# A decoder layer's cross-attention: scores from the context itself, with W_q and W_k folded into one matrix

## The chip, the cores and the metric

The kernel runs on one core of a Trainium2 chip. The metric is the device time of one execution in microseconds. The engines are named as the profile names them: PE (TensorE, matmuls), PEld (PE's weight loads, which run beside its matmuls), DVE (VectorE), ACT (ScalarE), POOL (GpSimd) and SP (SyncE, which issues most DMAs).

## The reference, cut to what matters

One decoder layer: a state-space scan block, a cross-attention over a context of 1601 rows, and a mixture of experts. Every tensor is fp32, the model width is 256. The part that the change touches is the cross-attention, which gets the layer-normed residual stream (2048 rows) as query:

```python
q = jnp.einsum('bse,ae->bsa', query, Wq) + bq
k = jnp.einsum('bse,ae->bsa', key, Wk) + bk        # key is the context, 1601 x 256
v = jnp.einsum('bse,ae->bsa', value, Wv) + bv      # value is the context too
scores = jnp.einsum('bqa,bka->bqk', q, k) / scale  # scale is 16
scores = jnp.where(mask == 0, jnp.float32(-10000000000.0), scores)
attn = jax.nn.softmax(scores, axis=-1)
return jnp.einsum('bqk,bka->bqa', attn, v)
```

## The kernel before, in words

The program has two blocks one after the other, with every engine's instructions written out in order and tied together by semaphores. `scan_block` fills the first 431 us of the span. `attend_and_route` does the rest: a prologue, the attention loop, the dense part of the experts with the routing, and the expert tiles. Nothing of the second block starts before the first has ended.

**Precision.** Large products are made from two fp32r halves. A value x is split as x_hi (rounded to fp32r by ACT when it evicts a PSUM bank) and x_lo = x - x_hi (by DVE, from the same bank). `products` (L1289) then issues three matmuls, hi by hi, hi by lo and lo by hi. Other products, such as the query projection (L1399), are one fp32 matmul, which the trace lists as two matmul records with two weight loads.

**The prologue.** It works through a list, `items` (L771), of PSUM banks to be filled by PE (`take`, L1297), evicted by ACT (L977 to L985) and halved by DVE (L1196 to L1209), always in the order of the list: the three weights, transposed (L1426); the context, transposed in eight pieces (L1434); the keys k = W_k c + b_k in eight pieces (L1437 to L1444); the values in thirteen pieces (L1453). At the start of the keys DVE also does `moments` (L1045): the last four of the sixteen row tiles get their statistics (L1047), and sixteen aggregations give mean and variance (L1051). POOL makes the inverse deviations of all rows from them (L861, L863), and DVE normalises the first query tile (`xn2`, L1186). Between keys and values stands `lead_at`: there every engine runs steps -2 and -1 of the loop, which is the transpose of xn2 (L1392), its eviction (L948), the query product (L1399), and the eviction and halving of q (L953, L1181).

**The attention loop.** `step(i)` is run for i = 0 to 17 on every engine; each handles one tile of 128 query rows in several phases. PE's order in a step is: transposes of the probabilities of tile i-1, groups 0 and 1 (L1321); transposes of the new row tile for the experts (L1344); the first 512 columns of scores of tile i; transposes of groups 2 and 3; transposes of the next query tile (L1392); the other score columns, 512, 512 and 66; the query product for tile i+1 (L1399); the product of the probabilities of tile i-1 with the values, 39 matmuls in thirteen groups of three (L1411). After steps 6, 10 and 14 come the router's logits of four tiles (L1355), after steps 8, 12 and 16 its ranks (L1364, L1366).

DVE's order in a step is: p_lo for the groups of tile i-1 (L1061); the residual of tile i-2 and its statistics (L1154 to L1162); the scores of tile i copied under the mask, in two pieces (L1168); their maximum (L1170); the bias -max/16 (L1172, `nb`); the normalised row of tile i-2 (L1176); q_lo of tile i+1 (L1181); xn2 of tile i+2 (L1186); parts of the routing in some steps. ACT evicts p_hi (L928), the transposes and q_hi (L953), and then does the exponential of tile i with the row sum as accumulator output (L963), which waits for `nb` and for which PE waits before the transposes of the next step (L1310).

SP loads the mask tiles (L815), the first of them once the transposed context has left the memory that the mask takes. POOL adds the value bias, fills the score buffer for the mask, and does the two small operations for the deviations (L901, L903).

## Time and profile before

| what | value |
|---|---|
| median of 3 runs | 826.59 us (825.5 to 828.36) |
| the profiled execution | 824.91 us |
| its span in the profile | 823.1 us, 11006 instructions |
| mean granted clock of PE | 0.883 |
| PE busy | 637.5 us (77%), 3196 matmuls |
| PEld busy | 400.5 us (49%) |
| DVE busy | 601.7 us (73%), 1009 |
| ACT busy | 421.6 us (51%), 744 |
| POOL busy | 453.6 us (55%), 324 |

The span is the profile's time from the first to the last instruction; the execution's own time is 1.8 us longer. Times in the rows are microseconds from the start of the span, and a row of the timeline merges like instructions that follow each other (x8 is eight of them). The duration of a matmul includes its way through the array, so the pace of a row of matmuls is read from their starts. What stands in brackets at the end of a row is the engine's idle time before it, and what ended it. The granted clock is given as a share of 2.4 GHz.

### The profile page before, as it was taken

Reading aid. Unit: us, or ns where it says so; the run is one execution under the profiler, and the core shown is the slowest. Engines: PE = TensorE matmul, PEld = TensorE weight load, DVE = VectorE, ACT = ScalarE, POOL = GpSimd, SP = SyncE. Lnnn points to the kernel's source line nnn. Section 1 sums busy time; section 2 is a strip of 40 time slices with the busy share of each in tenths; the row PEclk is TensorE's granted clock in tenths of the full one; section 3 lists DMA queues with packets and bytes.
Section 4 is the critical chain, followed back from the end, with each engine's and each line's share of the span. In section 5 each row is a group of like instructions: output and inputs, shape, how many; then the busy total and the mean of one; then the engine's idle time right before and its main releaser. Section 6 shows DMA issues by size and latency. Waiting matters only on the chain. (4 is left out here: it accounts for less than half of the span.)

```text
span 823.1 us, 11006 instructions
## 1 busy us (share of the span) xinstructions
PE 637.5 (77%) x3196; PEld 400.5 (49%) x3196; DVE 601.7 (73%) x1009; ACT 421.6 (51%) x744; POOL 453.6 (55%) x324
## 2 busy tenths in 40 slices
PE   4569857996499854653379799999999988899950
PEld 2123212341134210210038699998989964588840
DVE  5767787799977999997987566668777665344316
ACT  2557898587966898553425334434334220244420
POOL 3058698798986989995942212212334236046550
PEclk9789986999689985675589899999999999999985
DMA  7143342334334344464202113313413049655418
GB/s 195 34 109 92 76 99 64 97 87 102 88 79 99 78 105 103 100 186 103 67 0 87 41 61 111 131 46 128 144 54 106 15 133 325 139 152 150 134 27 300
DMA packets 70584, 87.43 MB, mean 106 GB/s; under 512 B 18197, under 2 KB 47320, under 8 KB 70526
## 3 DMA queue, kind: packets, MB, share of 16 engines
q1 hardware_dynamic: 54782, 67.26, 30.7%
q10 hardware_dynamic: 12000, 11.28, 4.3%
q0 software_dynamic: 3744, 8.19, 2.9%
q8 instruction: 27, 0.44, 0.2%
q14 instruction: 31, 0.25, 0.1%
HBM read 36.54 MB, written 18.66 MB: 67 GB/s over the span
## 5 line engine op out<-in xcount | busy, mean ns | idle before, releaser
L262 POOL TENSOR_TENSOR b_in<-u_rep,b_rep 128x1024 f32<-128x1024 f32 x128 | 299.0, 2361 | 72.3 <-DMA dt_rep<-dt 30.1
L477 DVE TENSOR_TENSOR_SCAN h<-ps,hlast,b_in 128x512 f32<-128x512 f32 x256 | 306.3, 1265 | 22.0 <-ACT ps L383 11.1
L383 ACT ACTIVATE ps<-dt_rep,neg_a 128x512 f32<-128x512 f32 x256 | 171.4, 686 | 75.5 <-DVE h L477 60.2
L615 PE MATMUL ps<-h,pick 128*32 128x512 f32 x512 | 84.9, 742 | 70.4 <-DVE h L477 70.0
L512 PE MATMUL ps<-xnT,w_in 128*128 128x512 f32 x128 | 67.8, 677 | 17.6 <-ACT xnT L308 10.3
L615 PEld LDWEIGHTS ps<-h,pick 128*32 128x32 f32 x512 | 11.0, 118 | 134.9 <-DVE h L477 130.5
L917 POOL DMA_INDIRECT rows_by_token<-yt,yrow x46 | 44.9, 975 | 52.4 <-DVE yrow L1254 25.3
L1061 DVE TENSOR_TENSOR p_lo<-ps,p_hi 128x512 fp32r<-128x512 f32 x64 | 35.1, 587 | 42.8 <-ACT p_hi L928 42.6
L1292 PE MATMUL ps<-v_hi,p_hi 128*128 128x256 f32 x208 | 59.7, 287 | 1.2 <-DVE x_res L1158 1.2
L1292 PE MATMUL ps<-v_hi,p_lo 128*128 128x256 f32 x208 | 58.5, 281 | 0.0
L1292 PE MATMUL ps<-v_lo,p_hi 128*128 128x256 f32 x208 | 58.5, 281 | 0.0
L928 ACT ACTIVATE p_hi<-ps 128x512 fp32r<-128x512 f32 x64 | 30.0, 516 | 45.4 <-PE ps L1321 45.4
L512 PEld LDWEIGHTS ps<-xnT,w_in 128*128 128x128 f32 x128 | 26.1, 214 | 55.3 <-issue 37.6
L895 POOL TENSOR_TENSOR x_res<-x_res,bv 128x256 f32<-128x256 f32 x16 | 11.7, 734 | 68.5 <-ACT pr L963 68.5
L1292 PE MATMUL ps<-k_hi,q_hi 128*128 128x512 f32 (+1 forms) x128 | 48.4, 378 | 1.0 <-ACT v_hi L983 1.0
L901 POOL TENSOR_TENSOR rstd3s<-mv3s,eps 128x1 f32<-128x1 f32 x16 | 3.1, 191 | 81.6 <-DVE mv3s L1162 81.6
L1292 PE MATMUL ps<-k_lo,q_hi 128*128 128x512 f32 (+1 forms) x128 | 46.9, 366 | 0.0
L1292 PE MATMUL ps<-k_hi,q_lo 128*128 128x512 f32 (+1 forms) x128 | 46.6, 367 | 0.0
L527 PE MATMUL ps<-xp,conv_d 128*128 128x512 f32 x96 | 43.6, 598 | 0.0
L1537 PE MATMUL ps<-w_exp,xT 128*128 x184 | 43.5, 379 | 0.0
L963 ACT ACTIVATE pr<-sc,nb 128x1601 f32<-128x1601 f32 x16 | 26.2, 1640 | 28.1 <-DVE nb L1172 28.1
L1292 PEld LDWEIGHTS ps<-v_hi,p_hi 128*128 128x128 f32 x208 | 39.3, 189 | 1.4 <-DVE x_res L1158 1.4
(228 smaller groups left out, 1289.3 us busy)
## 6 DMA issues: line engine op xcount, KB each, us to landing
u_rep<-u SPq DMA_DIRECT2D x256, 64.0 KB, 2.0
dt_rep<-dt SPq DMA_DIRECT2D x248, 64.0 KB, 2.0
mask_sb<-in_mask_BxSxS_ik_dram SPq DMA_DIRECT2D x16, 800.5 KB, 4.5
xt<-rows_by_expert SPq DMA_DIRECT2D x46, 129.0 KB
rows_by_token<-pad ACTq DMA_DIRECT2D x4, 1024.0 KB, 5.1
yb<-rows_by_token SPq DMA_DIRECT2D x4, 512.0 KB, 5.2
yb<-rows_by_token ACTq DMA_DIRECT2D x4, 512.0 KB, 5.9
x_res<-in_x_dram SPq DMA_DIRECT2D x1, 1536.0 KB, 8.7
```

The costliest lines, as they stand in the source:

```text
L262: pool.tensor_tensor(b_in[:, (t - 1) % NB:(t - 1) % NB + 2, :], u_rep[:, n % 2, j - 1:j + 1, :], b_rep[:, q % 2, g, :].unsqueeze(1).to_bro ...
L383: act.activation(psA[:, t % NDA, :], dt_rep[:, n % 2, j, :], ACT.Exp, scale=neg_a[:, k:k + 1]).then_inc(exp_ready, 1)
L477: dve.tensor_tensor_scan(h[:, QC * (s % NH) + j, :], psA[:, t % NDA, :], b_in[:, t % NB, :], hlast[:, k:k + 1], ALU.mult, ALU.add).then_in ...
L512: last = pe.matmul(psF[:, m % 2, :], w_in[:, n, part * DI + m * P:part * DI + (m + 1) * P], xnT[:, n, :], start=(n == 0), stop=(n == KE - 1))
L527: last = pe.matmul(psF[:, m % 2, :], conv_d[:, m, n, :], xp[:, m, n:n + CH], start=(n == 0), stop=(n == NTAP - 1))
L615: last = pe.matmul(psY[32 * j:32 * j + 32, :], pick[:, :], h[:, QC * (s % NH) + j, :], start=False, stop=(g == NG - 1))
L917: pool.indirect_dma_start(y_dram[:, :], bass.IndirectOffsetOnAxis(ap=yrow[:, 2 * s + a:2 * s + a + 1], axis=0), yt[:, s % YT, a, :], None, ...
L928: act.activation(p_hi[:, (i - 1) % 2, a:b, :], psP[g % 2][:, 0:(b - a) * P], ACT.Copy).then_inc(pthi_ready, 1)
L963: act.activation(pr[:, par, 0:SK], sc[:, par, :], ACT.Exp, bias=nb[:, par:par + 1], scale=SCALE, accum_out=rs[:, par:par + 1]).then_inc(ex ...
L1061: dve.tensor_tensor(p_lo[:, (i - 1) % 2, a:b, :], psP[g % 2][:, 0:(b - a) * P], p_hi[:, (i - 1) % 2, a:b, :].bitcast(F32), ALU.subtract).t ...
L1292: mm = pe.matmul(out, stat[a], mov[b], start=first and n == 0, stop=last and n == 2)
L1537: last = pe.matmul(psG[i % 2][:, a * 2 * FI:(a + 1) * 2 * FI], xT[:, i % 2, cols], w_all[:, ds(e, 1), wcols].rearrange("p a n -> p (a n)") ...
```

## The change

The scores are taken as (W_k^T (W_q x + b_q)) . c instead of q . k. With `wqk` = W_q^T W_k (made by PE in fp32 from the weights as loaded, without transposes) and W_k^T b_q as the bias of the new query, c is the transposed context, which the kernel holds in halves already. The term q . b_k is the same for a whole row of scores and leaves the softmax unchanged; it is still computed for each row (`qb`, a product with the vector W_q^T b_k and a sum along the row on DVE) and goes through max and bias as (qb - (max + qb))/16. What the diff does:

- `items` loses the transposes of W_q and W_k and the eight pieces of keys, and gets two items after the context: `wqk`, and `fold`, which holds W_q^T b_k on all partitions, b_q . b_k, and W_k^T b_q. Both are evicted by ACT alone.
- The 66 last context columns are also kept as whole fp32 (`c_end`, two small copies by DVE), and the last 66 score columns are two fp32 matmuls in place of six fp32r ones.
- The query is evicted as fp32 `q` by two ACT instructions; a third, from `q`, makes `q_hi`. DVE makes `q_lo` with one subtraction of 256 columns. PE waits for `q` where it waited for `q_lo` before it reuses the bank of the query.
- DVE gets in each tile, between the masked copy and the maximum, a scalar_tensor_tensor of 257 columns with an accumulator output, and after the maximum a tensor_tensor of one column, on which `nb` waits.
- `moments` stands where the fold items come, after the halving of the context. `c_hi` and `c_lo` stay in memory through the loop where `k_hi` and `k_lo` were.

The diff, cut to its core:

```diff
@@ -702,13 +702,14 @@
         with ExitStack() as first:
-            k_hi, k_lo = sb("k_hi", [P, KE, SKP], F32R, first), sb("k_lo", [P, KE, SKP], F32R, first)
+            c_hi, c_lo = sb("c_hi", [P, KE, SKP], F32R, first), sb("c_lo", [P, KE, SKP], F32R, first)
+            c_end = sb("c_end", [P, KE, SCOL[-1][1] - SCOL[-1][0]], F32, first)
+            fold = sb("fold", [P, 2 + DM + KE], F32, first)
             v_hi, v_lo = sb("v_hi", [P, KC, DM], F32R, first), sb("v_lo", [P, KC, DM], F32R, first)
             xqT = sb("xqT", [P, KE, P], F32, first)
-            q_hi, q_lo = sb("q_hi", [P, 2, KE, P], F32R, first), sb("q_lo", [P, 2, KE, P], F32R, first)
+            q, q_hi, q_lo = sb("q", [P, 2, KE, P], F32, first), sb("q_hi", [P, 2, KE, P], F32R, first), sb("q_lo", [P, 2, KE, P], F32R, first)
+            qb, full, prod = sb("qb", [P, 1], F32, first), sb("full", [P, 1], F32, first), sb("prod", [P, DM + 1], F32, first)
             with ExitStack() as prep:
-                c_hi, c_lo = sb("c_hi", [P, KE, SKP], F32R, prep), sb("c_lo", [P, KE, SKP], F32R, prep)
-                wk_hi, wk_lo = sb("wk_hi", [P, KE, DM], F32R, prep), sb("wk_lo", [P, KE, DM], F32R, prep)
                 wv_hi, wv_lo = sb("wv_hi", [P, KE, DM], F32R, prep), sb("wv_lo", [P, KE, DM], F32R, prep)
@@ -759,19 +762,21 @@
-        wq_items = [(bank[0].rearrange("p (k n) -> p k n", k=KE), wqT[:, :, :], None, None)]
-        wkv_items = [(bank[n].rearrange("p (k n) -> p k n", k=KE), hi[:, :, :], lo[:, :, :], None)
-                     for n, (hi, lo) in ((1, (wk_hi, wk_lo)), (2, (wv_hi, wv_lo)))]
-        ctx_items = [(bank[(3 + n) % 8][:, 0:b - a], c_hi[:, k, a:b], c_lo[:, k, a:b], None)
+        wv_items = [(bank[0].rearrange("p (k n) -> p k n", k=KE), wv_hi[:, :, :], wv_lo[:, :, :], None)]
+        ctx_items = [(bank[(1 + n) % 8][:, 0:b - a], c_hi[:, k, a:b], c_lo[:, k, a:b], c_end[:, k, :] if b == SKP else None)
                      for n, (k, (a, b)) in enumerate([(k, ab) for ab in KCOL for k in range(KE)])]
-        k_items = [(bank[(3 + n) % 8][:, 0:b - a], k_hi[:, m, a:b], k_lo[:, m, a:b], bk[:, m:m + 1])
-                   for n, (m, (a, b)) in enumerate([(m, ab) for ab in KCOL for m in range(KE)])]
+        fold_items = [(bank[1].rearrange("p (k n) -> p k n", k=KE), wqk[:, :, :], None, None),
+                      (bank[2][:, 0:1 + DM + KE], fold[:, 0:1 + DM + KE], None, None)]
         VBANKS = (3, 4, 5, 7, 0, 1, 2)
         v_items = [(bank[VBANKS[n % 7]][:, 0:DM], v_hi[:, n, :], v_lo[:, n, :], None) for n in range(KC)]
-        items = wq_items + wkv_items + ctx_items + k_items + v_items
+        items = wv_items + ctx_items + fold_items + v_items
         lead_at = len(items) - len(v_items)
-        bank_of = ([0, 1, 2] + [(3 + j) % 8 for j in range(len(ctx_items))] + [(3 + j) % 8 for j in range(len(k_items))]
-                   + [VBANKS[j % 7] for j in range(len(v_items))])
+        bank_of = [0] + [(1 + j) % 8 for j in range(len(ctx_items))] + [1, 2] + [VBANKS[j % 7] for j in range(len(v_items))]
+        fold_at = len(wv_items) + len(ctx_items)
+
+        def halved(n):
+            return len([lo for _, _, lo, _ in items[:n + 1] if lo is not None])
+
         cv_src = [bank[k][:, 0:KS * P].rearrange("p (t n) -> p t n", t=KS) for k in range(KE)]
@@ -814,7 +819,7 @@
-            sp_.wait_ge(prep_ps, 3 + len(ctx_items))
+            sp_.wait_ge(prep_ps, fold_at)
             for i in range(NT):
@@ -950,8 +955,11 @@
                     for m in range(KE):
-                        act.activation(q_hi[:, (i + 1) % 2, m, :], psA[:, (KE + m) * P:(KE + m + 1) * P], ACT.Identity,
-                                       bias=bq[:, m:m + 1]).then_inc(qhi_ready, 1)
+                        last = act.activation(q[:, (i + 1) % 2, m, :], psA[:, (KE + m) * P:(KE + m + 1) * P], ACT.Identity,
+                                              bias=fold[:, DM + 1 + m:DM + 2 + m])
+                    last.then_inc(q_ready, 1)
+                    act.wait_ge(q_ready, i + 2)
+                    act.activation(q_hi[:, (i + 1) % 2, :, :], q[:, (i + 1) % 2, :, :], ACT.Copy).then_inc(qhi_ready, 1)
                 if on(i, 0):
@@ -974,15 +982,13 @@
             act.wait_ge(b_in, 48)
-            for n, (src, hi, lo, bias) in enumerate(items):
+            for n, (src, hi, lo, whole) in enumerate(items):
                 if n == lead_at:
+                    act.wait_ge(prep_hi, lead_at)
                     step(-2)
...
                 act.wait_ge(prep_ps, n + 1)
-                if bias is None:
-                    act.activation(hi, src, ACT.Copy).then_inc(prep_hi, 1)
-                else:
-                    act.activation(hi, src, ACT.Identity, bias=bias).then_inc(prep_hi, 1)
+                act.activation(hi, src, ACT.Copy).then_inc(prep_hi, 1)
             for i in range(NT + 2):
@@ -1041,6 +1047,7 @@
             dve.memset(x3[:, :, 0:KS - 1], 0.0)
+            dve.memset(xn2[:, :, DM:DM + 1], 1.0)
@@ -1166,24 +1173,31 @@
                         dve.copy_predicated(sc[:, par, a:b], mask_sb[:, par, a:b], psS[:, a:b]).then_inc(masked, 1)
+                    if i == 0:
+                        dve.wait_ge(prep_hi, lead_at)
+                    dve.wait_ge(xn2_ready, i + 1)
+                    dve.scalar_tensor_tensor(prod[:, :], xn2[:, par, :], 1.0, fold[:, 0:DM + 1], ALU.mult, ALU.mult,
+                                             accum_out=qb[:, :]).then_inc(qb_ready, 1)
                     dve.wait_ge(masked, 2 * i + 2)
                     dve.reduce_max(mx[:, par:par + 1], sc[:, par, :], AXX).then_inc(dve_link, 1)
+                    dve.wait_ge(qb_ready, i + 1)
                     dve.wait_ge(dve_link, i + 2)
-                    dve.tensor_scalar(nb[:, par:par + 1], mx[:, par:par + 1], -SCALE, None, ALU.mult).then_inc(nb_ready, 1)
+                    dve.tensor_tensor(full[:, :], mx[:, par:par + 1], qb[:, :], ALU.add).then_inc(full_ready, 1)
+                    dve.wait_ge(full_ready, i + 1)
+                    dve.tensor_scalar(nb[:, par:par + 1], qb[:, :], full[:, 0:1], SCALE, ALU.subtract, ALU.mult).then_inc(nb_ready, 1)
                 if on(i, -2):
...
                 if on(i, 1):
-                    dve.wait_ge(qhi_ready, KE * (i + 2))
-                    for m in range(KE):
-                        dve.scalar_tensor_tensor(q_lo[:, (i + 1) % 2, m, :], psA[:, (KE + m) * P:(KE + m + 1) * P], bq[:, m:m + 1],
-                                                 q_hi[:, (i + 1) % 2, m, :].bitcast(F32), ALU.add, ALU.subtract).then_inc(qlo_ready, 1)
+                    dve.wait_ge(qhi_ready, i + 2)
+                    dve.tensor_tensor(q_lo[:, (i + 1) % 2, :, :], q[:, (i + 1) % 2, :, :],
+                                      q_hi[:, (i + 1) % 2, :, :].bitcast(F32), ALU.subtract).then_inc(qlo_ready, 1)
                 if on(i, 2):
...
                         dve.wait_ge(xq_ps, i + 1)
-                    dve.tensor_scalar(xn2[:, par, :], x_res[:, i + 2, :], mv[:, i + 2, 0:1], rstd[:, i + 2:i + 3],
+                    dve.tensor_scalar(xn2[:, par, 0:DM], x_res[:, i + 2, :], mv[:, i + 2, 0:1], rstd[:, i + 2:i + 3],
                                       ALU.subtract, ALU.mult).then_inc(xn2_ready, 1)
@@ -1193,20 +1207,19 @@
-            for n, (src, hi, lo, bias) in enumerate(items):
+            for n, (src, hi, lo, whole) in enumerate(items):
+                if n == fold_at:
+                    moments()
                 if lo is None:
                     continue
-                if n == 3 + len(ctx_items):
-                    moments()
                 if n == lead_at:
...
                 dve.wait_ge(prep_hi, n + 1)
-                if bias is None:
-                    dve.tensor_tensor(lo, src, hi.bitcast(F32), ALU.subtract).then_inc(prep_lo, 1)
-                else:
-                    dve.scalar_tensor_tensor(lo, src, bias, hi.bitcast(F32), ALU.add, ALU.subtract).then_inc(prep_lo, 1)
+                if whole is not None:
+                    dve.tensor_copy(whole, src[:, 0:whole.shape[1]])
+                dve.tensor_tensor(lo, src, hi.bitcast(F32), ALU.subtract).then_inc(prep_lo, 1)
             for i in range(NT + 2):
@@ -1325,14 +1338,17 @@
                     if first == 0:
-                        pe.wait_ge(qlo_ready, KE * (i + 1))
+                        pe.wait_ge(qlo_ready, i + 1)
                     for s in range(first, last_):
...
                         for k in range(KE):
-                            last = products(psS[:, a:b], (q_hi[:, i % 2, k, :], q_lo[:, i % 2, k, :]),
-                                            (k_hi[:, k, a:b], k_lo[:, k, a:b]), k == 0, k == KE - 1)
+                            if s == len(SCOL) - 1:
+                                last = pe.matmul(psS[:, a:b], q[:, i % 2, k, :], c_end[:, k, :], start=(k == 0), stop=(k == KE - 1))
+                            else:
+                                last = products(psS[:, a:b], (q_hi[:, i % 2, k, :], q_lo[:, i % 2, k, :]),
+                                                (c_hi[:, k, a:b], c_lo[:, k, a:b]), k == 0, k == KE - 1)
                         if s % 2 == 1:
@@ -1378,7 +1394,7 @@
                     if on(i, 0):
-                        pe.wait_ge(qlo_ready, KE * (i + 1))
+                        pe.wait_ge(q_ready, i + 1)
                     x3_transposed(i - 3)
@@ -1386,7 +1402,7 @@
                     if i >= 0:
-                        pe.wait_ge(qlo_ready, KE * (i + 1))
+                        pe.wait_ge(q_ready, i + 1)
                     pe.wait_ge(xn2_ready, i + 2)
@@ -1396,7 +1412,7 @@
                         for k in range(KE):
-                            last = pe.matmul(psA[:, (KE + m) * P:(KE + m + 1) * P], wqT[:, k, m * P:(m + 1) * P], xqT[:, k, :],
+                            last = pe.matmul(psA[:, (KE + m) * P:(KE + m + 1) * P], wqk[:, k, m * P:(m + 1) * P], xqT[:, k, :],
                                              start=(k == 0), stop=(k == KE - 1))
@@ -1419,12 +1435,11 @@
             pe.wait_ge(w_in, 48)
-            for m in range(3):
-                out_ = take()
-                for a in range(KE):
-                    for k in range(KE):
-                        last = pe.transpose(out_[:, k, a * P:(a + 1) * P], w_raw[:, m, a, k * P:(k + 1) * P], ident[:, :])
-                last.then_inc(prep_ps, 1)
+            out_ = take()
+            for a in range(KE):
+                for k in range(KE):
+                    last = pe.transpose(out_[:, k, a * P:(a + 1) * P], w_raw[:, 2, a, k * P:(k + 1) * P], ident[:, :])
+            last.then_inc(prep_ps, 1)
@@ -1434,28 +1449,39 @@
-            for g, (a, b) in enumerate(KCOL):
-                pe.wait_ge(prep_lo, 2 + KE * (g + 1))
-                for m in range(KE):
-                    out_ = take()
-                    for k in range(KE):
-                        last = products(out_, (wk_hi[:, k, m * P:(m + 1) * P], wk_lo[:, k, m * P:(m + 1) * P]),
-                                        (c_hi[:, k, a:b], c_lo[:, k, a:b]), k == 0, k == KE - 1)
-                    last.then_inc(prep_ps, 1)
+            out_ = take()
+            for k in range(KE):
+                for a in range(KE):
+                    last = pe.matmul(out_[:, k, :], w_raw[:, 0, a, k * P:(k + 1) * P], w_raw[:, 1, a, :], start=(a == 0), stop=(a == KE - 1))
+            last.then_inc(prep_ps, 1)
+            pe.wait_ge(b_in, 48)
+            out_ = take()
+            for a in range(KE):
+                pe.matmul(out_[:, 0:DM], bk[:, a:a + 1].to_broadcast([P, P]), w_raw[:, 0, a, :], start=(a == 0), stop=(a == KE - 1))
+            for a in range(KE):
+                pe.matmul(out_[:, DM:DM + 1], bk[:, a:a + 1].to_broadcast([P, P]), bq[:, a:a + 1], start=(a == 0), stop=(a == KE - 1))
+            for m in range(KE):
+                for a in range(KE):
+                    last = pe.matmul(out_[:, DM + 1 + m:DM + 2 + m], w_raw[:, 1, a, m * P:(m + 1) * P], bq[:, a:a + 1],
+                                     start=(a == 0), stop=(a == KE - 1))
+            last.then_inc(prep_ps, 1)
             for c in range(KC):
...
                     pe.wait_ge(prep_hi, q_last + 1)
-                    pe.wait_ge(prep_lo, q_last)
+                    if halved(q_last):
+                        pe.wait_ge(prep_lo, halved(q_last))
+                    pe.wait_ge(prep_hi, lead_at)
                     step(-2)
                     step(-1)
+                pe.wait_ge(prep_lo, halved(fold_at))
                 out_ = take()
...
             pe.wait_ge(prep_hi, len(items))
-            pe.wait_ge(prep_lo, len(items) - 1)
+            pe.wait_ge(prep_lo, halved(len(items)))
             for i in range(NT + 2):
```

## Rows read from the trace of the kernel before

**Rows 1.** Windows: busy us (count) of PE, PEld, DVE, ACT, POOL; clock; DMA.
```profile
459.50:667.00 207.50, 199.69 (x1419) 183.59 (x1419) 146.69 (x336) 75.85 (x158) 56.74 (x74) 0.98 0.26 87
...
431.80:447.00 15.20, 14.08 (x86) 12.28 (x86) 12.77 (x40) 9.67 (x19) 4.36 (x12) 1.00 0.31 117
```

**Rows 2.** Timeline of the prologue, all engines: start, us, engine, line, operation.
```profile
432.53 0.60 ACT L983 ACTIVATE wqT<-ps 128x512 f32<-128x512 f32 x1 [10.59 <-PE ps L1426]
...
433.14 3.00 PE L1434 MATMUL ps<-ident,c_raw 128*128 128x128 f32 x26
...
433.65 0.69 DVE L1207 TENSOR_TENSOR wk_lo<-ps,wk_hi 128x512 fp32r<-128x512 f32 x1 [1.75 <-ACT wk_hi L983]
...
434.86 4.07 DVE L1207 TENSOR_TENSOR c_lo<-ps,c_hi 128x512 fp32r<-128x512 f32 x8
...
438.84 1.40 DVE L1047 BATCH_NORM_STATS2 stats<-x_res 128x6 f32<-128x256 f32 x4
...
441.89 2.93 POOL L863 TENSOR_TENSOR attn_rstd<-attn_rstd,attn_powers 128x16 f32<-128x16 f32 x1
...
446.64 0.41 DVE L1186 TENSOR_SCALAR xn<-x_res,attn_mv,attn_rstd 128x256 f32<-128x256 f32 x1
...
447.19 0.41 PE L1392 MATMUL ps<-ident,xn 128*128 128x128 f32 x2 [1.26 <-DVE xn L1186]
...
448.08 1.16 PE L1399 MATMUL ps<-xqT,wqT 128*128 128x128 f32 x8 [0.47 <-ACT xqT L948]
```

**Rows 3.** Timeline of one tile of the attention loop, all engines.
```profile
507.76 0.90 PEld L1321 LDWEIGHTS ps<-ident,pr 128*128 128x128 f32 x8
...
513.69 2.00 DVE L1168 COPY_PREDICATED sc<-mask_sb,ps 128x1024 f32<-128x1024 int32 x2
...
515.72 1.82 DVE L1170 TENSOR_REDUCE mx<-sc 128x1 f32<-128x1601 f32 x1
...
517.58 0.15 DVE L1172 TENSOR_SCALAR nb<-mx 128x1 f32<-128x1 f32 x1
...
517.66 0.42 DVE L1176 TENSOR_SCALAR xn<-x_res,mv3s,rstd3s 128x256 f32<-128x256 f32 x1
...
517.77 1.64 ACT L963 ACTIVATE pr<-sc,nb 128x1601 f32<-128x1601 f32 x1 [1.54 <-DVE nb L1172]
...
519.31 0.18 ACT L963 ACTIVATION_READ_ACCUMULATOR pr<-sc,nb 128x1 f32 x1
...
519.91 0.90 PEld L1321 LDWEIGHTS ps<-ident,pr 128*128 128x128 f32 x8
```

**Rows 4.** Timeline where the loop's last tile begins.
```profile
660.20 1.64 ACT L963 ACTIVATE pr<-sc,nb 128x1601 f32<-128x1601 f32 x1 [6.04 <-DVE nb L1172]
...
661.98 0.86 PEld L1321 LDWEIGHTS ps<-ident,pr 128*128 128x128 f32 x8 [0.68 <-ACT pr L963]
```

**Rows 5.** Waits in the loop: engine, line, releaser: us, times, longest.
```profile
PEld ps L1321 <- ACT pr L963: 4.6, 2, 3.9
```

**Rows 6.** PE timeline of another tile: a 66-column product, the query product, the logits.
```profile
590.23 0.28 PE L1292 MATMUL ps<-k_lo,q_hi 128*128 128x66 f32 x1
...
590.78 1.14 PE L1399 MATMUL ps<-xqT,wqT 128*128 128x128 f32 x8
...
596.37 1.86 PE L1355 MATMUL ps<-r_w,x 128*128 128x16 f32 x16
```

**Rows 7.** Groups by line and form: busy us, mean ns, then idle.
```profile
L1244 DVE SCALAR_TENSOR_TENSOR x_res<-xn,w_same,x_res 128x256 f32<-128x256 f32 x16 | 7.6, 477 | 0.0
```

**Rows 8.** Timeline of the scan's end: four fp32 products of 256 columns.
```profile
429.02 1.99 PE L540 MATMUL ps<-w_out,zs 128*128 128x256 f32 x8 [0.81 <-DVE zs L434]
```

**Rows 9.** Windows around PE's wait in the first tile, columns as in rows 1.
```profile
467.00:469.00 2.00, 0.00 (x0) 0.00 (x0) 1.46 (x5) 1.31 (x1) 0.00 (x0) 0.61 0.81 330
...
474.00:475.00 1.00, 1.00 (x8) 0.99 (x8) 0.00 (x0) 0.33 (x1) 0.00 (x0) 0.86 0.00 0
```

**Rows 10.** Timeline of the same place.
```profile
469.47 1.97 PE L1321 MATMUL ps<-ident,pr 128*128 128x128 f32 x8 [3.73 <-ACT pr L963]
```

18 lines of the change are left out of this document (10 added, 8 removed).

## The prediction

> **What bounds the kernel now.** I first split the attention block by windows [rows 1]. In the loop, from 459.5 to 667 us, PE is busy 199.7 of 207.5 us and DVE only 146.7, so the loop is PE's. In the prologue, 431.8 to 447, PE is busy 14.1 of 15.2 us, but DVE 12.8, so it may be either's. Busy shares don't settle what ends last in a stage; the timelines do.
>
> In the prologue [rows 2] PE ends the context's transposes at 433.14 + 3.00 = 436.14, issues the keys until 447.19 - 1.26 = 445.93, and stands 1.26 us for `xn2` (DVE, 446.64). Beside the keys runs a second chain: DVE halves the context (434.86 to 438.93), does the moments (from 438.84), POOL raises to the power -1/2 (441.89 to 444.82, one instruction of 2.93 us), DVE normalises. That chain would have had `xn2` ready soon after 444.8; DVE was then still halving keys. So the keys end last, but the moments chain ends only 1.8 us before them. This is what I look for: the work removed covers something almost as long.
>
> In the loop [rows 3] a tile takes 519.91 - 507.76 = 12.15 us on PE. A second chain closes on itself in each tile: probability transposes, p_hi, p_lo, masked copy, maximum, `nb`, exponential, next transposes. Where this chain is known to bind [rows 4], PE starts 661.98 - 660.20 = 1.78 us after the exponential starts. In the tile of rows 3 the exponential starts at 517.77, so PE could have started at 519.55 and started at 519.91: **slack 0.37 us**. The waits say the same: PE's weight loads stood for the exponential in 2 tiles only, the first and the last [rows 5]. Of the 15 intervals between the 16 tiles' probability transposes, 3 hold the logits (1.86 us of PE work on top [rows 6]), one is the slow tile after the first, 2 are ends, and 9 are like the one shown within 0.05 us or, where routing comes in on DVE, somewhat longer.
>
> **Part 1, the prologue.** Removed on PE: eight weight transposes and the keys. From the pace of row L1434 (26 in 3.00 us, 0.115 each) the transposes are 0.9 us; the keys are 445.93 - 436.14 = 9.8 us. Added: six fp32 products of 256 columns and six of one column. Four of the former took 1.99 us [rows 8], so six are at most 3.0 us; one of the latter costs at least its two weight loads and at most the 0.28 us of two records at L1399's pace (1.14 us for 8 [rows 6]), 1.7 us in all. PE would then be ready for `xn2` at 445.93 - 0.9 - 9.8 + 4.7 = 439.9. By PE's work alone the prologue gains 7.3 us.
>
> But `xn2` isn't there. DVE's first operation now starts when ACT's first eviction ends, 432.53 + 0.60 = 433.13, and one halving instead of two lies before the context's. Two took 434.86 - 433.65 = 1.21, so the context's halving starts at 433.15 + 0.60 = 433.75, 1.1 us earlier. The two `c_end` copies of 66 columns take back 0.15 us each at `nb`'s price of 0.15 for a tiny operation [rows 3]; at most 0.28. The rest of the chain is unchanged and now has no cover: the moments begin 0.8 us earlier, POOL ends at 444.0, `xn2` starts at 444.1 instead of 446.64. **Gain 2.5 us** (2.3 to 2.8), with PE standing idle from 439.9 to about 444.6. ACT loses two weight and eight key evictions and gets two; it has nothing on this path. SP's mask loads start 0.9 us earlier and nobody waits for them.
>
> **What that idle time costs.** In the first tile PE stops at 469.47 - 3.73 = 465.74 [rows 10], and the granted clock falls from full (2.4 GHz) to half (1.2 GHz) at about 467.4, since its mean is 0.61 from 467 to 469 [rows 9]. PE works again at 469.47 and the clock is back at about 474.3 (mean 0.86 from 474 to 475). A wait of 3.7 us thus brought 4.8 us at half clock. The new wait is 4.7 us, so I expect the same: half clock until 444.6 + 4.8 = 449.4. The dense work (query product, then values) starts 0.9 us after the transposes as now (448.08 against 447.19), so 3.9 us are worked at half clock, which loses 1.95, and 0.15 for the transposes: **2.1 us given back**. Bounds: 0, if the clock holds, and 3.3 us, if the half clock lasts half as long again. Part 1 nets -0.4 us.
>
> **Part 2, the loop on PE.** Six fp32r matmuls of 66 columns start 0.11 us apart ((590.78 - 590.23)/5 [rows 6]): 0.66. The new two are four records. The eight 128-column records of L1399 take 1.14 with 0.28 for the last, so 0.12 each; with 66 columns they are no slower: 0.48. **PE saves 0.2 us a tile** (0.15 to 0.4). PE's earlier release by `q` instead of `q_lo` is worth nothing: q_lo was ready long before PE came to it.
>
> **Part 3, the loop on DVE.** Between the masked copy and the exponential come two operations. The scalar_tensor_tensor's nearest row is L1244, two fp32 operands in SBUF, 256 columns: 0.477 [rows 7]. It waits for nothing, so it overlaps its predecessor by the 0.07 us that DVE rows show when no wait is between (`nb` ends at 517.73, the next has started at 517.66 [rows 3]), and its successor by as much, where the maximum today starts 0.03 after the copy (513.69 + 2.00, 515.72): net 0.29. No row of DVE has an accumulator output. ACT's has one, and there it leaves a second instruction of 0.18 us that ends 0.08 after the main one ([rows 3], 519.31 + 0.18 against 517.77 + 1.64). I add 0.07; the bounds are 0 and 0.18. The Trainium skill says the same of DVE: an operation that writes its accumulator is two instructions (VectorE: DVE Perf Modes, Two Vector instructions with no wait between them). The one-column addition costs `nb`'s 0.15 + 0.04 for the wait: 0.19, as `nb` to exponential shows (517.77 - 517.58). **D = 0.29 + 0.07 + 0.19 = 0.55 us** later at the exponential; bounds 0.48 and 0.75.
>
> q_lo becomes one operation instead of two, but stands behind `nb` and shortens nothing there. The third ACT instruction for the query falls into ACT's wait of 1.54 us for `nb` [rows 3]; it reads 256 columns, and even at the 0.60 of the prologue's 512-column eviction [rows 2] none of it shows. If `nb` came 1 us earlier, it would.
>
> **The sum of the loop.** D exceeds the slack of 0.37, so the exponential becomes the last to arrive in ordinary tiles. Per interval: the 9 ordinary ones and the slow tile, taken as ordinary, D - 0.37 = +0.18 each, 10 x 0.18 = +1.8. The 3 with logits keep PE as bound: -0.6. The first end: D - 0.2 = +0.35. The last: D = +0.55. Together **+2.1 us**. With part 1: **+1.7 us** on the profiled 824.91, so 826.6. That execution lies 1.7 us under the median of the runs, 826.59; for the median I add the same: 828.3. A measurement of this kernel can tell about 0.3% (2.5 us) from no change.
>
> **Rivals.**
> *The clock holds* through PE's wait (or falls near its end): the loss of 2.1 goes, sum -0.4, 826.2. Against it: the fall came 1.7 us into a shorter wait [rows 9, 10]. It is no change too.
> *PE stays the bound* (faster). If D is 0.37 or less, or the slack is larger than the rows show, 0.2 x 16 = -3.2 us in the loop; with part 1 at -0.4 to -2.5 the time is 821 to 823. Against it: the maximum, `nb` and exponential stand one behind the other with no gap to take up 0.48 us between them.
> *The whole of the keys is gained* (faster): the prologue gives 7.3 instead of 2.5, with no wait and no lost clock: -7.3 + 2.1 = -5.2, 821.4. That needs the moments chain off the path; against it, POOL's one instruction of 2.93 us starts after DVE's whole halving.
> *DVE's new operation is slow* (slower). The place is between copy and maximum. If two fp32 SBUF operands with a running sum went at half the pace of L1244, it would last 0.95, D would be 1.03 and the loop 10 x 0.66 - 0.6 + 0.83 + 1.03 = +7.9; sum +7.5, 834.1. It decides from D = 0.65 on: 10 x 0.28 - 0.6 + 0.45 + 0.65 = +3.3, less 0.4. For it: nothing in the trace shows this operation with its sum. Against: L1244 has the two operands and takes 0.477, where `nb`'s 0.15 and 256 columns at the maximum's pace (1.82/1601 = 1.14 ns) make 0.44. The Trainium skill has this rule: such an operation with two SBUF sources that aren't bf16 has half the throughput (Vector Engine (DVE) Microarchitecture Reference, Points that are easy to get wrong); L1244 contradicts it without a sum, and no row here shows it with one.
>
> **How the numbers follow.** Forecast and the clock rival, both within 2.5 us: 0.38 and 0.17. Slow DVE work, or the forecast's terms at their upper bounds (D 0.75: 10 x 0.38 - 0.6 + 0.55 + 0.75 = +4.5; 3.3 lost to the clock: +0.8; sum +5.3): 0.30. PE as bound 0.09, whole gain 0.06. So faster 0.15, same 0.55, slower 0.30. The range leaves out the whole gain, the strongest PE-bound case and doubled DVE price: from 823.5 (D at 0.48, PE's saving 0.4, 2.8 gained in the prologue and the clock held make 10 x 0.11 - 1.2 + 0.1 + 0.5 - 2.8 = -2.3, or 824.3, with 0.8 for the runs' own spread) to 832.0 (the terms at their upper bounds).
>
> **What would show it.** In the profile after: `xn2` at 444.1, PE idle for some 4.5 us before it, granted clock 0.5 in the window behind it; the value products' start at about 447; PE's weight loads of the probabilities released by the exponential in 10 or more tiles instead of 2; a tile of 12.3 us, the maximum starting some 0.4 us after the copy's end; four records between the last 512 columns and the query product. I'm wrong if the tile is 11.95 us (PE still binds) or over 12.5 us (D was too small), and if PE finds `xn2` ready.

## The result and the profile after

The kernel after takes 828.31 us (median of 20 runs, 825.64 to 832.93) against 825.45 (20 runs, 822.67 to 828.36): **ratio 1.0041, 95% interval 1.0029 to 1.0054**, 3.4 us slower (2.4 to 4.5). A second set of runs of the same program gave 1.0038 [1.0019, 1.0056], where 1.0025 to 1.0045 was expected. The profiled execution took 827.98 us. Head of its page:

```profile
span 826.3 us, 10924 instructions
...
PE 636.8 (77%) x3132; PEld 395.5 (48%) x3132; DVE 601.4 (73%) x1035; ACT 422.8 (51%) x752; POOL 453.8 (55%) x324
```

I read it by stretches: the prologue (first weight transpose to first score product on PE), the first scores (to the first probability transpose), the loop (to the last tile's first transpose), and what lies before and behind.

| us | start | prologue | first scores | loop | behind |
|---|---|---|---|---|---|
| before | 431.81 | 27.75 | 9.91 | 192.51 | 161.17 |
| after | 434.85 | 27.13 | 10.26 | 194.92 | 159.09 |
| after, second set | 432.48 | 27.34 | 10.25 | 195.00 | 160.35 |

Start and behind hold the same work in every kernel here and still wander between executions (431.8 to 434.9, and 159.1 to 162.9). The three stretches between make **-0.62 + 0.35 + 2.41 = +2.14 us**.

**The prologue**, timeline of the kernel after (start, us, engine, line), to be set beside [rows 2]:

```profile
436.81 3.67 DVE L1222 TENSOR_TENSOR c_lo<-ps,c_hi 128x512 fp32r<-128x512 f32 x6
...
441.06 1.40 DVE L1054 BATCH_NORM_STATS2 stats<-x_res 128x6 f32<-128x256 f32 x4
441.11 1.03 PE L1465 MATMUL ps<-bq,w_qkv_raw 128*128 128x1 f32 x8
...
444.10 2.93 POOL L868 TENSOR_TENSOR attn_rstd<-attn_rstd,attn_powers 128x16 f32<-128x16 f32 x1
447.06 0.41 DVE L1200 TENSOR_SCALAR xn<-x_res,attn_mv,attn_rstd 128x256 f32<-128x256 f32 x1 [3.41 <-POOL attn_rstd L868]
447.62 0.66 PE L1408 MATMUL ps<-ident,xn 128*128 128x128 f32 x2 [5.49 <-DVE xn L1200]
448.82 2.07 PE L1415 MATMUL ps<-xqT,wqk 128*128 128x128 f32 x8 [0.53 <-ACT xqT L953]
```

PE is done at 442.1 and stands 5.49 us for `xn2`; what the keys covered is now the path. Behind the wait the query product takes 2.07 us instead of 1.16 [rows 2], and the windows show why (columns as in [rows 1], the granted clock third from the end): half clock, 1.2 of 2.4 GHz, where [rows 1] have 1.00:

```profile
446.00:448.00 2.00, 0.38 (x2) 0.29 (x2) 0.41 (x1) 0.00 (x0) 1.93 (x7) 0.51 0.00 0
448.00:452.00 4.00, 3.47 (x17) 3.19 (x16) 0.00 (x0) 1.42 (x4) 0.22 (x3) 0.50 0.00 0
452.00:454.00 2.00, 2.00 (x15) 2.00 (x15) 1.37 (x4) 0.77 (x4) 0.00 (x0) 0.78 0.00 0
```

**An ordinary tile**, to be set beside [rows 3]:

```profile
504.09 2.00 DVE L1175 COPY_PREDICATED sc<-mask_sb,ps 128x1024 f32<-128x1024 int32 x2
...
505.98 0.41 DVE L1179 SCALAR_TENSOR_TENSOR prod<-xn,fold 128x257 f32<-128x257 f32 x1
506.32 0.08 DVE L1179 DVE_READ_ACCUMULATOR prod<-xn,fold 128x1 f32 x1
506.32 1.82 DVE L1182 TENSOR_REDUCE mx<-sc 128x1 f32<-128x1601 f32 x1
...
508.24 0.16 DVE L1185 TENSOR_TENSOR full<-mx,qb 128x1 f32<-128x1 f32 x1
508.43 0.21 DVE L1187 TENSOR_SCALAR nb<-qb,full 128x1 f32<-128x1 f32 x1
...
508.68 1.64 ACT L971 ACTIVATE pr<-sc,nb 128x1601 f32<-128x1601 f32 x1 [1.76 <-DVE nb L1187]
```

From the copy's start to the exponential's are 508.68 - 504.09 = 4.59 us, against 4.08 before: **D = 0.51 us**. The maximum now starts 0.23 after the copy's end instead of 0.03, and from its end to the exponential are 0.54 instead of 0.23. Waits of the loop, to be set beside [rows 5]:

```profile
PEld ps L1334 <- ACT pr L971: 7.5, 10, 4.5
...
PE ps L1334 <- DVE base L1117: 2.1, 2, 1.0
```

The exponential holds PE in 10 tiles instead of 2; `base`, the last routing operation that uses the shared PSUM bank, holds it for 2.1 us in all where it was 0.8.

**The loop's 15 intervals** between first probability transposes, after minus before:

| kind | how many | before | after | change, sum |
|---|---|---|---|---|
| the slow one behind the first tile | 1 | 14.27 | 13.97 | -0.30 |
| ordinary | 6 | 11.94 to 12.34 | 11.98 to 12.36 | +0.37 |
| with logits on PE | 3 | 13.87 to 13.89 | 13.78 to 13.83 | -0.18 |
| with routing on DVE, first of a pair | 2 | 13.02, 13.06 | 13.37, 13.37 | +0.65 |
| with routing on DVE, second of a pair | 2 | 12.80, 12.76 | 13.46, 13.48 | +1.38 |
| the last | 1 | 11.86 | 12.35 | +0.49 |

A pair is two intervals in a row, over which DVE does the routing of four tiles. Of +2.41 us, 2.03 fall into the four intervals with routing. **What binds there**, first the kernel before, then after (timelines of the first pair; the last row is PE at the beginning of the second interval):

```profile
557.65 0.18 ACT L963 ACTIVATION_READ_ACCUMULATOR pr<-sc,nb 128x1 f32 x1
...
558.39 1.04 PE L1321 MATMUL ps<-ident,pr 128*128 128x128 f32 x8
558.53 1.53 DVE L1081 CAST at_f<-top_at 128x8 f32<-128x8 uint32 x1
558.59 1.45 POOL L897 MEMSET sc<- 128x1601 f32 x1
...
560.63 1.28 DVE L1061 TENSOR_TENSOR p_lo<-ps,p_hi 128x512 fp32r<-128x512 f32 x2
...
561.37 0.93 PE L1321 MATMUL ps<-ident,pr 128*128 128x128 f32 x5 [0.35 <-DVE p_lo L1061]
...
568.85 1.64 ACT L963 ACTIVATE pr<-sc,nb 128x1601 f32<-128x1601 f32 x1 [1.38 <-DVE nb L1172]
...
572.45 0.63 PE L1321 MATMUL ps<-ident,pr 128*128 128x128 f32 x4 [0.40 <-DVE base L1110]
```

```profile
560.88 0.18 ACT L971 ACTIVATION_READ_ACCUMULATOR pr<-sc,nb 128x1 f32 x1
...
561.12 1.09 PE L1334 MATMUL ps<-ident,pr 128*128 128x128 f32 x8
...
561.56 1.70 DVE L1088 CAST at_f<-top_at 128x8 f32<-128x8 uint32 x1
561.80 1.44 POOL L902 MEMSET sc<- 128x1601 f32 x1
563.30 0.36 DVE L1092 TENSOR_TENSOR hot<-ids,at_f 128x64 f32<-128x64 f32 x2
...
563.84 1.28 DVE L1068 TENSOR_TENSOR p_lo<-ps,p_hi 128x512 fp32r<-128x512 f32 x2
...
564.58 0.93 PE L1334 MATMUL ps<-ident,pr 128*128 128x128 f32 x5 [0.74 <-DVE p_lo L1068]
...
572.56 1.64 ACT L971 ACTIVATE pr<-sc,nb 128x1601 f32<-128x1601 f32 x1 [1.59 <-DVE nb L1187]
...
576.14 0.63 PE L1334 MATMUL ps<-ident,pr 128*128 128x128 f32 x4 [1.02 <-DVE base L1117]
```

A cast of 8 columns takes 1.5 to 1.7 us, and in both kernels it ends with POOL's memset: 560.06 against 560.04, 563.26 against 563.24. The Trainium skill gives the rule (SBUF — State Buffer, SBUF: two separate sides): VectorE, in its two-port mode, and GpSimd lock a shared pair of ports for a whole instruction, and the other waits. The trace agrees as to the waiting; in which mode the cast ran no row says. But by these records the cast begins ahead of the memset that holds it, by 0.06 us before and 0.24 after. The memset follows the end of the exponential (561.06 + 0.74), so the cast, all of DVE's stream behind it, and the first `p_lo` stand at a fixed distance behind the exponential. Before, the exponential had ended 0.56 us ahead of PE's transposes (557.83 against 558.39), now 0.06. So `p_lo` starts 2.72 us behind the transposes instead of 2.24, 0.48 later, nearly all of D, and PE waits 0.74 us for it instead of 0.35. In the same tile D comes a second time: the next exponential starts 11.44 us behind those transposes instead of 10.46. What is late by then stays late until `base`, for which PE waits 1.02 instead of 0.40 us. The two intervals together grow by 1.01 us, which is twice D.

### The profile page after: what moved, and what is told of

Read it like the earlier page. It is cut to its first block and busy times, and to the rows that moved or that the text cites. A ratio compares the mean times of both kernels' runs of the same rounds, so it can differ in the third digit from the quotient of the medians.

```text
span 826.3 us, 10924 instructions
## 1 busy us (share of the span) xinstructions
PE 636.8 (77%) x3132; PEld 395.5 (48%) x3132; DVE 601.4 (73%) x1035; ACT 422.8 (51%) x752; POOL 453.8 (55%) x324
## 5 line engine op out<-in xcount | busy, mean ns | idle before, releaser
L615 PE MATMUL ps<-h,pick 128*32 128x512 f32 x512 | 87.9, 766 | 68.9 <-DVE h L477 68.5
L1305 PE MATMUL ps<-c_hi,q_hi 128*128 128x512 f32 x96 | 41.1, 428 | 1.0 <-ACT v_hi L991 1.0
L612 PE MATMUL ps<-xc,skip_d 128*128 128x512 f32 x32 | 23.4, 821 | 22.0 <-DVE zs L434 22.0
L1305 PEld LDWEIGHTS ps<-v_lo,p_hi 128*128 128x128 f32 x208 | 39.3, 189 | 0.0
```

What stands on the lines that cost most here:

```text
L615: last = pe.matmul(psY[32 * j:32 * j + 32, :], pick[:, :], h[:, QC * (s % NH) + j, :], start=False, stop=(g == NG - 1))
L1305: mm = pe.matmul(out, stat[a], mov[b], start=first and n == 0, stop=last and n == 2)
```

## The experiments

All ratios are against the kernel before, of five rounds each; stretches are from each run's profile.

**1. Is it the new addresses?** The kernel before, with `xn2` one column wider, as the change makes it.

```diff
-            xn2 = sb("xn2", [P, 2, DM], F32, second)
+            xn2 = sb("xn2", [P, 2, DM + 1], F32, second)
```

> The kernel before, with xn2 one column wider (257) and otherwise the same, so that every SBUF tile allocated behind it sits 8 bytes further on, as in the kernel after. Theory A (the change costs time only through DVE's chain in the loop and the wait in the prologue): ratio 1.000 within 0.1%. Rival B (the scan block, which the change doesn't touch, slowed by the shifted tiles, as its 434.8 us against 431.8 in the two profiles could suggest): +0.15 to +0.4%, and a scan block that ends near 434.8 us in the profile.

Measured: 825.07 us, ratio 1.0002 [0.9985, 1.0019], loop 192.77. The shift explains nothing. Its prologue took 29.26 us, though, 1.5 more than before's with the same instructions: the clock fell behind the wait of 1.25 us, which it had not done in the profile of before.

**2. The uncovered chain.** The kernel after, with the moments first on DVE.

```diff
+            moments()
             for n, (src, hi, lo, whole) in enumerate(items):
-                if n == fold_at:
-                    moments()
```

> The kernel after, with DVE's moments ahead of the halving of the context instead of behind it. Theory A: POOL's 2.93 us instruction now runs beside the halving; the halving ends some 1.5 us later, xn2 is ready 4.5 us earlier than in the kernel after, PE's wait of 5.5 us shrinks to 1 us, the granted clock stays at 1.00 through the prologue, which saves a further 2 us. 6 to 7 us faster than after, so 3 to 4 us faster than before: ratio 0.9955 to 0.997. Rival C (PE's wait in the prologue covers nothing that matters, because DVE's halving or the values' evictions take its place): no more than 2 us faster than after, ratio 1.001 to 1.004. Rival D (the wait counts, the clock doesn't): 4.5 us, ratio 0.9985.

Measured: 821.09 us, ratio **0.9948 [0.9929, 0.9968]**, prologue 21.06 us instead of 27.13. Its timeline:

```profile
435.95 2.93 POOL L868 TENSOR_TENSOR attn_rstd<-attn_rstd,attn_powers 128x16 f32<-128x16 f32 x1
...
440.24 0.41 DVE L1200 TENSOR_SCALAR xn<-x_res,attn_mv,attn_rstd 128x256 f32<-128x256 f32 x1
...
441.56 0.41 PE L1407 MATMUL ps<-ident,xn 128*128 128x128 f32 x2 [0.68 <-ACT fold L991]
...
442.50 1.16 PE L1414 MATMUL ps<-xqT,wqk 128*128 128x128 f32 x8 [0.53 <-ACT xqT L953]
```

`xn2` is ready at 440.65, before PE comes to it at 441.56, and the clock stays full in this execution. The prologue takes 6.7 us less than before's, nearly the 7.3 that the prediction gave for PE alone (6.0 us of work and the wait of 1.3). The ratio came out a little better than the 0.9955 to 0.997 expected; the loop of this execution is 1.4 us shorter than that of after, by the two things named in experiment 4.

**3. The same edit in the kernel before**, where the keys should cover that chain.

```diff
+            moments()
             for n, (src, hi, lo, bias) in enumerate(items):
...
-                if n == 3 + len(ctx_items):
-                    moments()
```

> The kernel before with the moments ahead of the halving of the weights, nothing else. My theory: in the kernel before the keys end last and only cover the moments chain, so freeing that chain takes away at most PE's wait of 1.26 us for xn2 and moves nothing else in the loop: ratio 0.998 to 1.000, xn2 on DVE still behind the halving of the last keys. Rival: the order of the moments is worth as much without the change (the 6 us that it gave in the kernel after, a gain from the clock and from something in the loop): ratio 0.993 to 0.995; then the change has nothing to do with it.

Measured: 826.82 us, ratio 1.0009 [0.9992, 1.0027]. PE's wait is the same to the hundredth:

```profile
447.22 1.32 DVE L1208 SCALAR_TENSOR_TENSOR k_lo<-ps,bk,k_hi 128x512 fp32r<-128x512 f32 x3 [0.61 <-ACT k_hi L985]
448.46 0.40 DVE L1186 TENSOR_SCALAR xn<-x_res,attn_mv,attn_rstd 128x256 f32<-128x256 f32 x1
449.01 0.41 PE L1391 MATMUL ps<-ident,xn 128*128 128x128 f32 x2 [1.26 <-DVE xn L1186]
```

DVE was on the keys until then, whatever the moments did. The edit even costs something here: the halvings stand behind the moments, and `xn2` starts 15.51 us into the block (448.46 - 432.95) instead of 14.83. So the edit of 2 is worth nothing without the change: the gain there is the change's own, and only the new order lets it through.

**4. The clock.** The kernel after, with 11 fp32 products of 256 columns, whose result nobody reads, in PE's wait.

```diff
+                    pe.wait_ge(prep_hi, 4)
+                    pe.wait_ge(prep_lo, 4)
+                    for r in range(11):
+                        pe.matmul(bank[3][:, 0:DM], w_raw[:, 0, 0, 0:P], w_raw[:, 1, 0, :], start=True, stop=True)
                     pe.wait_ge(prep_hi, lead_at)
                     step(-2)
```

> The kernel after, with eleven fp32 matmuls of 256 columns (results not used, into a free bank) put into PE's wait for xn2 in the prologue, 4.7 us of work in a wait of 5.5. If the half clock behind that wait costs what the forecast said (Theory A: 2.1 us), the granted clock reads 1.00 from 440 to 456 us, xn2 and its transposes stand where they stood in after, the values are through some 2 us earlier, ratio 1.0015 to 1.0025 against before. Rival F (the clock falls there by chance anyway, in before too, since the profile of the padded kernel before shows 0.93 from 435 to 459 where before shows 1.00): on average less than 1 us gained, ratio 1.003 to 1.004.

Measured: 824.28 us, ratio 0.9984 [0.9973, 0.9996]; the granted clock is 1.00 throughout the prologue, which takes 25.22 us: **the clock costs 27.13 - 25.22 = 1.9 us** there. The total gained 4.0 us, more than the 2 expected. In the profiled execution two things outside the prologue make up the rest; whether they are in the other runs too isn't known. The slow interval took 13.28 instead of 13.97 (clock 0.93 instead of 0.87 from 459 to 485), and the first interval with routing 12.27 instead of 13.37, because the cast this once got by:

```profile
558.42 0.34 DVE L1088 CAST at_f<-top_at 128x8 f32<-128x8 uint32 x1
...
558.67 1.47 POOL L902 MEMSET sc<- 128x1601 f32 x1
559.07 1.10 DVE L1094 COPY xn<-at_f 128x4 f32<-128x4 f32 x1
```

The small copy behind it is then the one held (to 560.17, memset to 560.14), and nobody waits for that. The same happened once in experiment 2. In the other 26 of 28 such places of all the profiles the cast was held. The start of the cast doesn't tell which it will be: by the records' starts to the nanosecond, it got by 0.239 and 0.249 us ahead of the memset, and was held at 0.237, at 0.249 (experiment 6) and at 0.255. **A hold costs this interval 1.1 us, and the pair 0.9**, since the next interval took 13.61 and 13.62 us in the two executions instead of 13.46. What it costs in the kernel before isn't shown, as the cast was held in each of its profiles.

**5. DVE's new work in the loop.** The kernel after without it; left out is the term q . b_k, the same for a whole row of scores.

```diff
-                    dve.scalar_tensor_tensor(prod[:, :], xn2[:, par, :], 1.0, fold[:, 0:DM + 1], ALU.mult, ALU.mult,
-                                             accum_out=qb[:, :]).then_inc(qb_ready, 1)
...
-                    dve.tensor_tensor(full[:, :], mx[:, par:par + 1], qb[:, :], ALU.add).then_inc(full_ready, 1)
-                    dve.wait_ge(full_ready, i + 1)
-                    dve.tensor_scalar(nb[:, par:par + 1], qb[:, :], full[:, 0:1], SCALE, ALU.subtract, ALU.mult).then_inc(nb_ready, 1)
+                    dve.tensor_scalar(nb[:, par:par + 1], mx[:, par:par + 1], -SCALE, None, ALU.mult).then_inc(nb_ready, 1)
```

> The kernel after without the term q.b_k: the scalar_tensor_tensor and the one-column addition between the masked copy and nb are gone, nb is -max/16 as before. What is left out is the same for a whole row of scores and leaves the softmax as it is. Theory A: the exponential comes 0.5 us earlier in each tile, PE is the bound again with 0.25 us less work a tile: a tile of 11.9 us against 12.26 in after and 12.17 in before; first to last transposes 4 to 5 us shorter than in after; 5 to 6 us faster than after, ratio 0.997 to 0.998 against before. Rival E (the two operations are hidden, the loss is elsewhere): as after, ratio 1.004.

Measured: 824.89 us, ratio 0.9994 [0.9976, 1.0013], loop 191.26, 3.7 us less than after. Ordinary intervals like the one shown fall to 12.03, those with routing to 13.05 and 12.82, as before. So D makes the loop's loss, in both kinds of interval. An ordinary tile of 11.9 was expected, since PE's saving was taken as 0.25 us; 12.03 against 12.17 before make it 0.13. The ratio gained 1 to 2 us less than expected.

**6. Twice the suspect.** The kernel after, with the scalar_tensor_tensor issued twice, the first into tiles that nobody reads.

```diff
+                    dve.wait_ge(qb2_ready, i)
+                    dve.scalar_tensor_tensor(prod2[:, 0:DM + 1], xn2[:, par, :], 1.0, fold[:, 0:DM + 1], ALU.mult, ALU.mult,
+                                             accum_out=qb2[:, 0:1]).then_inc(qb2_ready, 1)
                     dve.scalar_tensor_tensor(prod[:, :], xn2[:, par, :], 1.0, fold[:, 0:DM + 1], ALU.mult, ALU.mult,
```

> The kernel after, with the scalar_tensor_tensor and its accumulator output issued twice between masked copy and maximum. Theory A: the chain binds, so each of the 12 intervals without logits grows by the whole price of one, 0.34 to 0.42 us, a tile of 12.6 to 12.7 us, first to last transposes 4.5 to 5.5 us longer than in after: ratio 1.0095 to 1.011 against before. Rival E (DVE has room there): ratio 1.004 to 1.005.

Measured: 831.26 us, ratio 1.0063 [1.0047, 1.0080], loop 198.61 (+3.7). Ordinary intervals take 12.62 instead of 12.26: with no slack left each 0.35 us on DVE (the second starts 0.35 behind the first) is 0.36 of the tile. A pair with routing grows by 0.72 us, twice the 0.36. The intervals with logits gave nothing (13.74 against 13.78 in the first; PE still binds there), and the whole is less than the 4.5 to 5.5 us expected, by the loop and more so by the ratio (1.0095 to 1.011 expected).

**7. The exact term off the path** (r8). Moments first, and the scalar_tensor_tensor of the next tile at the end of the step, behind `xn2`.

```diff
-                    dve.scalar_tensor_tensor(prod[:, :], xn2[:, par, :], 1.0, fold[:, 0:DM + 1], ALU.mult, ALU.mult,
-                                             accum_out=qb[:, :]).then_inc(qb_ready, 1)
...
+                if on(i, 1):
...
+                    dve.scalar_tensor_tensor(prod[:, :], xn2[:, (i + 1) % 2, :], 1.0, fold[:, 0:DM + 1], ALU.mult, ALU.mult,
+                                             accum_out=qb[:, :]).then_inc(qb_ready, 1)
```

> All of the change kept, with two moves: the moments first (as in r2_moments), and the scalar_tensor_tensor for tile i+1 at the end of DVE's step i, in the 2.3 us in which DVE waits for the transposes of the probabilities. Only the one-column addition, 0.19 us, stays between maximum and exponential, less than the slack of 0.37. Theory A: PE binds in ordinary tiles, 12.0 to 12.05 us a tile as in r3_no_qb and r4_both, ratio 0.990 to 0.992 against before, level with r4_both. Rival H (the operation at the step's end pushes q_lo or the next p_lo): the tile is 12.2 us or more, ratio 0.994 or more.

Measured: 821.16 us, ratio 0.9937 [0.9913, 0.9961]. Less than expected: ordinary intervals fell to 12.08, but those with routing took 13.39 and 13.50, as in after. DVE's operation now stands in front of the routing. In the first of a pair the cast begins later, 0.08 us behind the memset, and ends with it all the same; the first `p_lo` starts 2.74 us behind PE's transposes, where it was 2.72 in after. In the second of a pair PE waits up to 1.3 us for `base` instead of 1.0.

**8. The 66 columns.** Six fp32r products again instead of the two fp32 ones, in the kernel after (r6) and in one without DVE's work and with the moments first (r4, the edits of 2 and 5 together; r9 with the six products).

```diff
-                            if s == len(SCOL) - 1:
+                            if s == len(SCOL):
```

> The kernel after, with the last 66 score columns as six fp32r matmuls again instead of two in fp32. Theory A (DVE's chain binds in ordinary tiles): PE's 0.2 us more a tile are taken from its wait for the exponential, a tile stays at 12.26 us, the three intervals with logits grow by 0.2; in all 0.3 to 1 us slower than after, ratio 1.0045 to 1.0055 against before. Rival G (PE still binds in after): 0.2 x 16 = 3.2 us slower, ratio 1.008.

> The last two edits together: moments first, and without the term q.b_k. Theory A: the two savings add, since they lie in different stretches: 11 to 12.5 us faster than after, 8 to 9.5 us faster than before, ratio 0.9885 to 0.990. Rivals C and E: the smaller of the savings is missing, ratio 0.996 or more.

> r4_both (moments first, no q.b_k), with the last 66 score columns as six fp32r matmuls again. Here PE binds in ordinary tiles, so the price of the 66 columns shows where in r6_six it was hidden. Theory A: the six records take 0.66 us where the four take 0.39 to 0.46, a tile of 12.2 us instead of 12.02, first to last transposes 2.5 to 3.5 us longer than r4_both's 190.5, ratio 0.993 to 0.995 against before. Rival I (the saving of the two fp32 matmuls is eaten elsewhere on PE): 12.05 us a tile, ratio 0.990 to 0.991.

Measured: r6 828.06 us, ratio 1.0021 [1.0004, 1.0038], loop 195.63 (+0.7), ordinary tile 12.26 as with the two. r4 817.50, ratio 0.9904 [0.9881, 0.9928], loop 190.51. r9 819.61, ratio 0.9932 [0.9910, 0.9954], loop 193.49: **+3.0 us**. Of these, 1.1 are the slow interval, 14.60 against 13.51, with the clock at 0.87 and 0.93 from 459 to 485 in the two executions, mostly the clock's and not the edit's. The other 1.9 are **0.2 in each of the six ordinary intervals and the three with logits**; the four with routing and the last one gained nothing. That the total fell into the 2.5 to 3.5 us expected is luck in part. PE's saving counts where PE binds and is hidden where the exponential or the routing does. In the kernel after it is mainly the intervals with logits that show it (13.96 against 13.81). By the ratio, r6 missed what was expected (1.0045 to 1.0055): its median is that of after, 828.06 against 828.31, and a difference of 0.7 us is too small to show there.

**9. Addresses once more.** The twelve score products of 512 columns took 2.89 us in after (525.95 to 528.84) and 2.82 before, with the same shapes; over all tiles of a profile the means are 2.88 and 2.84. So in r10 the kernel of r4 got its new tiles placed behind those that the kernel had before.

```diff
-            c_end = sb("c_end", [P, KE, SCOL[-1][1] - SCOL[-1][0]], F32, first)
-            fold = sb("fold", [P, 2 + DM + KE], F32, first)
             v_hi, v_lo = sb("v_hi", [P, KC, DM], F32R, first), sb("v_lo", [P, KC, DM], F32R, first)
...
+            q_hi, q_lo = sb("q_hi", [P, 2, KE, P], F32R, first), sb("q_lo", [P, 2, KE, P], F32R, first)
+            q = sb("q", [P, 2, KE, P], F32, first)
+            c_end = sb("c_end", [P, KE, SCOL[-1][1] - SCOL[-1][0]], F32, first)
```

> r4_both with the new tiles (q, c_end, fold) placed behind the old ones in SBUF, so that the values and the halves of the query lie in the same order as in before. In after and r4_both the twelve 512-column score matmuls of a tile take 2.88 us from the first to the next operation, in before 2.82. Rival J (the place in SBUF sets that pace): 2.82 us and a tile of 11.95 us, 1 us faster than r4_both. Rival K (it isn't the place): 2.88 us and the same time as r4_both, ratio 0.990.

Measured: 813.43 us, ratio **0.9862 [0.9838, 0.9887]**, the fastest version here, 11 us under before and 15 under after. Ordinary intervals fall from 12.02 to 11.94, the loop to 189.47. Its products run from the first to the second row below in 2.84 us:

```profile
529.33 0.48 PE L1297 MATMUL ps<-c_hi,q_hi 128*128 128x512 f32 x1
...
532.17 0.55 PE L1340 MATMUL ps<-c_end,q 128*128 128x66 f32 x4
532.56 1.11 PE L1407 MATMUL ps<-xqT,wqk 128*128 128x128 f32 x8
```

That is also their mean over its tiles, the pace of before. r6 and r9, with six products for the 66 columns in the old placing, stay at 2.88, so it isn't the two fp32 products that slow the twelve. Of the 4.1 us between the medians of r4 and r10, the profiles show 1.04 in the loop and 1.7 in the prologue, whose clock held in this execution and not in r4's. The first is the placing's, the second need not be, and the rest is not placed.

## Why the prediction was right, and where it was off

828.3 was forecast and 828.31 measured, which is closer than the reasoning deserves: it was made on the median of three runs, 826.59, and the larger set of before has 825.45. **As a difference I forecast +1.7 us; the profiles show +2.14, the runs +3.4 (2.4 to 4.5).** In its own numbers the profiled execution was forecast at 826.6 and took 827.98. The side, slower by a little, was right; whether by less or by more than the 0.3% that I set as the limit of no change, the interval (0.29% to 0.54%) all but decides for more. What the profiles don't hold of it, 1.3 us, I could not place; it is less than the wandering of the parts before and behind from one execution to the next.

**Part 1** held in all its steps. `xn2` started 447.06 - 434.85 = 12.21 us into the block instead of 446.64 - 431.81 = 14.83, 2.6 earlier (2.5 forecast), PE waited 5.5 us (4.7; the added products took 4.0 us and not 4.7), the clock fell, and gave back 1.9 us (2.1) by experiment 4. Net of the stretch -0.62 (-0.4). That net rests on one execution of before, in which the clock held; in experiments 1 and 3 it fell behind nearly the same wait and cost 1.5 us. Experiments 2 and 3 show the claim on which it stood, that the keys covered a chain almost as long. The rival "whole keys gained" failed on just that, and came about once the chain was moved.

**Part 2**: PE's saving was put at 0.2 us a tile. The four records take 0.39 us (0.48 forecast) against 0.59 (0.66), and some 0.05 are lost again in the twelve products before them, 2.88 against 2.84 on average, which no term held. Where PE binds, the net is 0.13 (experiment 5). Experiment 8 gives 0.2 for the edit alone.

**Part 3**: D was 0.51 (0.55): 0.20 between copy and maximum (0.36 forecast), 0.31 behind the maximum (0.19), since `nb` with two operands takes 0.21 instead of 0.15 and the first of the two starts 0.10 behind the maximum's end, where `nb` started 0.04 behind it. Two errors that cancelled. The working had slips of its own: its terms give 0.31 for the operation and not 0.29 (0.477 - 0.07 - 0.07 - 0.03), and of the upper bound of 0.75 they give 0.66. The slow rival fell at its first row: the operation takes 0.41 us, less than L1244's 0.477 [rows 7], sum and all, and the halved throughput of the Trainium skill's rule weighed there (Vector Engine (DVE) Microarchitecture Reference, Points that are easy to get wrong) doesn't show: a subtraction of 256 columns with two fp32 operands in SBUF takes 0.42 (`q_lo` of after). The accumulator is a second instruction, as the Trainium skill has it (VectorE: DVE Perf Modes, Two Vector instructions with no wait between them), but its 0.08 us lie wholly beside the maximum (both rows at 506.32).

**The step that failed is the sum of the loop.** It took "the 9 ordinary ones and the slow tile" alike at D minus a slack of 0.37, and so priced the four intervals with routing, which I had noted were longer, by a slack read in a tile without. There DVE's stream leaves none: 4 x 0.18 = 0.72 was forecast and 2.03 measured, twice D for each pair. (Ten intervals are of these two kinds, not nine; the count was short by one.) Against that stood 0.37 instead of 1.08 in the six ordinary ones, 0.06 each, so that their slack was on average 0.51 - 0.06 = 0.45 us instead of 0.37 (0.40 to 0.42 in the three like the tile read, more in the three others); -0.30 instead of +0.18 in the slow one, for which I have no row (the clock from 459 to 485 is 0.87 in both); -0.18 instead of -0.6 with logits. The two ends were right, +0.35 and +0.49 (0.35, 0.55). The sum was near because errors of both signs met, not because each term was.

What stays open: whether taking POOL's memset away from the cast gives the 1.1 us twice. It wasn't tried; the two executions in which the cast got by are the only evidence, and 0.15 of the 1.1 came back there in the next interval. Open too is why the slow interval shrank, and what decides whether the cast is held.

## What to carry to other kernels

Before pricing work that is removed, ask what it covered, and move the next chain before or with it: the same change was 0.4% slower alone and 0.5% faster with one call moved. Read the loop's intervals one by one before you put a difference of two profiles down to an edit: in experiment 8 more than a third of it was one interval at a lower clock. Slack belongs to one kind of interval; where a loop has several, read it in each, and price a delay in full where the delayed engine's own queue binds. A tiny operation with a duration many times its kind's can mark another engine that holds it; look for one that ends at the same time.
